# Two-layer cross attention on one core: the first layer's image-token softmax taken from the preparation into the attention's steps

## The reference

```
out_text = sdpa(q, k, v)                             # 1593 text tokens
out_ip   = sdpa(q, k_ip, v_ip, mask=mask_ip)         # 8 image tokens
out      = (out_text + out_ip) @ w_out + b_out + x   # the input of layer 2
```

## Time and profile before

| what | before |
|---|---|
| median of 3 runs | 1550.36 us (1549.09 to 1551.30) |
| the profiled execution's own time | 1552.15 us |
| its span in the profile | 1550.2 us |
| PE busy | 1456.7 us, 94% |
| DVE busy | 1119.9 us, 72% |
| ACT busy | 1060.8 us, 68% |
| POOL busy | 188.8 us, 12% |
| mean granted clock of PE, share of full | 0.969 |

### The profile page before, as it was taken

The page is one execution under the profiler, slowest core; times in us unless marked ns, Lnnn a source line. Parts: engine busy times, 40 slices in busy tenths (PEclk is TensorE's granted clock), DMA queues, the critical chain, the costliest instruction groups (busy, mean ns, idle before and its releaser), DMA issues. The chain is left out here.

```text
span 1550.2 us, 32737 instructions
## 1 busy us (share of the span) xinstructions
PE 1456.7 (94%) x12886; PEld 911.9 (59%) x12886; DVE 1119.9 (72%) x1572; ACT 1060.8 (68%) x1962; POOL 188.8 (12%) x363
## 2 busy tenths in 40 slices
PE   6797959999999999999999999999999999999995
PEld 4454513333333333477777777777777777777774
DVE  5777768887787877876767777777777777777625
ACT  2454538877877877767767777777777777777752
POOL 4653300000101101000010000000000000000000
PEclk9899959999999999899999999999999999999996
DMA  5266851221221212110011101100011001100000
GB/s 158 75 161 174 226 115 48 53 51 40 58 54 47 66 40 51 42 26 23 17 26 30 29 19 26 26 23 20 23 26 26 22 18 27 26 23 16 7 1 17
DMA packets 82902, 75.89 MB, mean 49 GB/s; under 512 B 28608, under 2 KB 70964, under 8 KB 82756
## 3 DMA queue, kind: packets, MB, share of 16 engines
q1 hardware_dynamic: 82756, 73.88, 18.3%
HBM read 47.73 MB, written 26.09 MB: 48 GB/s over the span
## 5 line engine op out<-in xcount | busy, mean ns | idle before, releaser
L1364 DVE TENSOR_TENSOR whole<-late,whole 128x1024 f16<-128x1024 f32 (+1 forms) x280 | 320.1, 1143 | 99.3 <-ACT whole L1223 96.2
L1349 DVE TENSOR_REDUCE mx<-ps_y 128x2 f32<-128x800 f32 (+2 forms) x227 | 223.9, 986 | 106.1 <-PE ps_y L1030 105.4
L1107 PE MATMUL ps_v<-eh,whole 128*128 128x269 f16 x1040 | 293.1, 282 | 0.0
L1107 PE MATMUL ps_n<-eh,whole 128*128 128x269 f16 x1040 | 291.6, 280 | 0.0
L1223 ACT CAST whole<-late 128x1024 f16<-128x1024 f32 (+1 forms) x280 | 275.6, 984 | 8.9
L1109 PE MATMUL ps_v<-el,whole 128*128 128x269 f16 x960 | 269.1, 280 | 0.0
L1110 PE MATMUL ps_v<-eh,whole 128*128 128x269 f16 x960 | 269.1, 280 | 0.0
L1110 PE MATMUL ps_n<-eh,whole 128*128 128x269 f16 x960 | 268.2, 279 | 0.0
L1109 PE MATMUL ps_n<-el,whole 128*128 128x269 f16 x960 | 268.1, 279 | 0.0
L1349 DVE TENSOR_REDUCE mx<-ps_x 128x2 f32<-128x800 f32 (+2 forms) x198 | 195.3, 987 | 82.0 <-PE ps_x L1030 81.1
L1349 DVE TENSOR_REDUCE mx<-ps_t 128x2 f32<-128x800 f32 (+2 forms) x215 | 211.4, 983 | 32.8 <-PE ps_t L1030 31.9
(11 more groups left out here) (433 smaller groups left out, 2072.9 us busy)
## 6 DMA issues: line engine op xcount, KB each, us to landing
e<-in_ctx SPq DMA_DIRECT2D x4, 1536.0 KB
kb<-k_parts SPq DMA_DIRECT2D x80, 74.9 KB
kb<-k_parts SPq DMA_DIRECT2D x80, 74.7 KB
k_parts<-kp SPq DMA_DIRECT2D x12, 400.0 KB
vb<-v_cols SPq DMA_DIRECT2D x40, 117.0 KB, 2.1
v_cols<-late SPq DMA_DIRECT2D x4, 1040.0 KB, 11.7
late<-v_cols SPq DMA_DIRECT2D x40, 104.0 KB, 2.0
qb<-q_parts SPq DMA_DIRECT2D x160, 25.0 KB
```

Source lines behind the costliest of these rows:

```text
L1107: pe.matmul(ps, hi, eh, start=(t == 0), stop=False)
L1349: nc.vector.tensor_reduce(mx[:, pair % 2, c, :], bank("max", pair, c)[:, :, 0:w], AX.X, ALU.max).then_inc(chunk_max, 1)
L1364: nc.vector.tensor_tensor(pl[s % 2][:, t0:t0 + w, :], ring[:, turn % EXPS, 0:w], ph[s % 2][:, t0:t0 + w, :], ALU.subtract).then_inc(low_do ...
```

## The change

`sc` of layer 0 leaves `queries` as before, but neither DVE nor ACT touches it in the preparation. In `attend` DVE makes one of the six operations at the end of each of steps 2, 3, 4, 6, 7 and 8, behind the reduce of p = 14 and ahead of the next step's p = 1; ACT makes the exponential at the end of step 5, behind the exponential of p = 12 and ahead of the copy in line 1256. An operation waits for the one before it by a semaphore; the reciprocal and the others keep their shapes. PE waits for the last of them ahead of stage `pT`. `mask` now lives as long as `sc`, and maximum and sum have small tiles of their own.

```diff
 STAGE0 = 1
+SOFTMAX_AT = (2, 3, 4, 6, 7, 8)
+EXP_SC_AT = 5
...
-                    if first:
-                        act.wait_ge(centred, 1)
-                        nc.scalar.activation(L["sc"][:], L["sc"][:], ACT.Exp).then_inc(exp_done, 1)
...
-                centre(nc.vector, link, L, 0, L["mask"], smax).then_inc(centred, 1)
...
-                    if first:
-                        dve.wait_ge(exp_done, 1)
-                        link(normalise(nc.vector, link, L, 0, None, ssum))
...
+        centring, exp_sc, norming = sem("centring"), sem("exp_sc"), sem("norming")
+        smax, ssum = sbuf("smax_0", [P, U * H], F32), sbuf("ssum_0", [P, U * H], F32)
+        sc0 = LS[0]["sc"][:].rearrange("p u (h n) -> p (u h) n", n=IP[0])
...
                     if name == "pT":
+                        pe.wait_ge(norming, 3)
...
+                    if s == EXP_SC_AT:
+                        act.wait_ge(centring, 3)
+                        nc.scalar.activation(LS[0]["sc"][:], LS[0]["sc"][:], ACT.Exp).then_inc(exp_sc, 1)
                     if stage_at(s):
...
+                def small_softmax(j):
+
+                    wide = [P, U * H, IP[0]]
+                    if j < 3:
+                        at_least(dve, centring, j)
+                    else:
+                        at_least(dve, norming, j - 3)
+                    if j == 0:
+                        for u in range(U):
+                            rows = LS[0]["sc"][:, u].rearrange("p (h n) -> p h n", n=IP[0])
+                            ins = nc.vector.tensor_tensor(rows, rows, LS[0]["mask"][:, u].to_broadcast([P, H, IP[0]]), ALU.add)
+                    elif j == 1:
+                        ins = nc.vector.tensor_reduce(smax[:], sc0, AX.X, ALU.max)
+                    elif j == 2:
+                        ins = nc.vector.tensor_tensor(sc0, sc0, smax[:].unsqueeze(2).to_broadcast(wide), ALU.subtract)
+                    elif j == 3:
+                        dve.wait_ge(exp_sc, 1)
+                        ins = nc.vector.tensor_reduce(ssum[:], sc0, AX.X, ALU.add)
+                    elif j == 4:
+                        ins = nc.vector.reciprocal(ssum[:], ssum[:])
+                    else:
+                        ins = nc.vector.tensor_tensor(sc0, sc0, ssum[:].unsqueeze(2).to_broadcast(wide), ALU.mult)
+                    ins.then_inc(centring if j < 3 else norming, 1)
...
                     low(s, NE - 1)
+                    if s in SOFTMAX_AT:
+                        small_softmax(SOFTMAX_AT.index(s))
                     if stage_at(s):
```

More of the change, by code:

```diff
@@ L122, in build @@
             ))
+        LS[0].update(mask=sbuf("mask", [P, U, 1, IP[0]], F32))
         LS[1].update(
@@ L131, in build @@
             L.update(parts=(sbuf("qp0", [P, 3, U * P], BF16, st), sbuf("qp1", [D - P, 3, U * P], BF16, st)),
-                     no_max=sbuf("no_max", [MROWS * H, U * P], BF16, st), mask=sbuf("mask", [P, U, 1, IP[0]], F32, st),
+                     no_max=sbuf("no_max", [MROWS * H, U * P], BF16, st),
                      vaug=vaug, vcut=vcut,
@@ L293, in prepare @@
         vh_done = sem("vh_done")
-        centred, exp_done, sm_step = sem("centred_0"), sem("exp_done_p"), sem("sm_step")
-        smax = K["res"][:, RR * KC:RR * KC + U * H]
-        ssum = K["n2"][:].rearrange("p g h -> p (g h)")[:, 0:U * H]
         eh_done, el_done = sem("eh_done"), sem("el_done")
@@ L1424, in centre @@
     sc = L["sc"]
[L1425 to L1431, removed]
+    link(vec.tensor_tensor(sc[:], sc[:], extra[:].rearrange("p u h n -> p u (h n)"), ALU.add))
     flat = sc[:].rearrange("p u (h n) -> p (u h) n", n=n)
```

## The result

The changed kernel takes **1554.29 us** (median of 10 runs, 1552.17 to 1558.50), the kernel before it 1550.34 in the same comparison (10 runs). The ratio is **1.0040**, with a 95% interval of 1.0028 to 1.0051: 4.3 to 7.9 us slower, 6.2 in the middle. The two medians lie 4.0 apart and the means of the two sets of ten 5.6; each set is spread over some 6 us, so the size is known no better than the interval says. The profiled execution took 1552.87 with a span of 1551.1.

The account below looks back on a forecast made before the run. The preparation was taken as a chain of waits, the attention as three engines passing work round three PSUM tiles. 6.36 + 0.7 - 2.5 = +4.6 us on the median 1550.36 gave 1555.0, range 1550.0 to 1558.8.

Parts of the forecast that it names:

- The two terms: Whole kernel: the preparation gets 2.5 us shorter, and the operations put into the attention add 7.06 us.
- The preparation: Batches 0 and 1: POOL's subtractions come earlier without DVE's softmax; gain 2.5 us, of which 1.6 from the front.
- Rival 2: Preparation: the softmax's two-input DVE operations hold POOL's first all-reduce, so up to 4.9 us comes back; 1552.6 us, chance 0.14.
- The attention: Steps 2 to 8: six DVE operations cost 6.36 us and ACT's exponential 0.7.
- the cover read from step 39: Attention, end of a step: slack before PE's score fill is late hides 0.37 us of each inserted DVE operation.
- ACT's exponential: Attention, end of step 5, ahead of ACT's copy: 1.18 us net, predicted cost 0.7, bounds 0 and 1.18.
- the two-step check in the prediction: Attention, plain step against step 39: reduce to score fill takes 2.55 us in both, so 0.36 inserted cost nothing.
- the granted clock: Attention steps with an operation: a fall below full clock would prove the forecast wrong; no size given.
- the bounds for the six operations: Attention: the six DVE operations cost between nothing (all covered by idle time) and 8.58 us (no cover).
- Rival 1: Attention: DVE's idle time, 1.5 us a step, covers the operations; 0 added, 2.5 gained, 1547.9 us, chance 0.13.

## Why the prediction was right

**The sign and the size.** It gave 4.6 us over the kernel before; measured are 6.2 (4.3 to 7.9). The 1555.0 lies 0.7 above the median of the changed kernel. The two terms that it had come to 6.7 - 2.6 = 4.1 by the runs, a little under that interval; the rest of the 6.2 fits a term that it left out (below).

**The preparation** (2.5 predicted, 2.6 measured with the softmax left out). The chain is the predicted one: the all-reduce stays behind POOL's configuration change (50.44, not 48), the second right behind it, the subtraction 1.8 earlier (1.6), ACT's first cast of batch 1 at 88.56 (89.5). Rival 2 is out with the first of these. The other profiles agree. From the first all-reduce to the first subtraction it is 9.56 to 9.95 in the three with the softmax in its old place and 7.66 to 8.02 in seven with it out; from that subtraction to batch 1's it is 39.18 to 40.00 and 38.46 to 39.01. That is 1.9 and 0.8 in the mean, where 1.6 and 0.9 were reckoned. The 6.1 by which the attention starts earlier in the two profiles is mostly the profiled execution of the kernel before. From DVE's first `eh` memset (38.58 there) to the attention's first `xT` memset (205.92) that execution took 167.3. The two profiles of the kernel with the operations made twice, which has the same preparation, took 163.2 and 163.5. Seven profiles with the softmax out of the preparation took 159.8 to 162.2, 161.3 in the mean: 2.1 less than these two. Most of the other 4.0 came in batches 2 and 3 of that one execution, where ACT's key casts wait for the landing of key DMAs.

**The attention** (7.06 predicted, 6.68 at full clock). The table has it term by term. The operations, each its duration less 0.08 and 0.37, came within 0.13 of every row at full clock, so the cover read from step 39 holds for whole operations. The one term off by more is ACT's exponential, 0.42 for 0.70. The prediction has the exponential behind the copy 0.89 late; it starts 2.32 after the last one of the step (274.86 to 277.18), in a plain step 1.66 (257.75 to 259.41), so it is 0.66 late. And PE's one wait of any size there isn't at that fill, but for the copy, at the product:

```profile
277.35 0.62 PE L1071 MATMUL ps_v<-whole,vb 128*9 128x256 f32 x8 [0.57 <-ACT acc L1245]
```

What the two-step check in the prediction could not see is that nothing is caught up later: only 0.14 comes back in the step behind the product.

**The term that was missing** is the granted clock. The sum took all steps at full clock. The text named a fall as something that would make it wrong, because no row had a stall of that length, but gave it no price; the bounds for the six operations ended at 8.58. It cost 1.3 to 2.7 in three of four profiles, 1.4 in the mean of the four; 4.1 and 1.4 make 5.5, within the interval. That the total came near without this term is in part luck: the spread of the runs is wider than the term, and an exponential 0.28 too dear made up for a little of it.

**Rival 1** failed for the place that the change chose, not in general. DVE's 1.5 us of idle time a step is real. In pieces put where it lies, the whole softmax cost nothing that shows (0.02 in steps 2 to 9).

## What to carry to other kernels

Where several engines pass tiles round a ring, an inserted operation cost its length less the waiting time at its own place, whatever the busy share of the engine said; read that place's gap from the timeline and cut the work to its size. What a step gives back is bounded by the next thing that isn't moved, here the time that another engine took from one kind of operation to the next, so look for the wait that will open there. Compare starts of stages over several profiles before a difference of two is taken for the change's: here 4 of 6 us were one execution's.

## What the runs showed of the hardware

- The granted clock fell to half after PE had waited 1.63 us in an otherwise busy stretch, in three of four profiles, and not in the fourth, after 1.62; once in twenty waits of 1.14 or 1.15; and after waits of 4.67 and of 3.85. In the kernels where PE never waited 0.9 us in steps 2 to 9 (softmax left out, behind the fold, in pieces) it stayed full. PE then worked at 1.2 GHz for about 3 to 8 us. What else decides it isn't shown.
- A two-input DVE operation of 1.49 us on SBUF held back a POOL subtraction that began under it by 1.2 us (2.15 to DVE's next block instead of 0.96); a one-input reduce of the same length, which also writes less, did not (1.05). The Trainium skill, SBUF — State Buffer, Who interferes with whom, says that a DVE instruction with two SBUF inputs contends with a GpSimd instruction that reads SBUF and that a tensor_reduce never does; these two rows agree.
- From the end of batch 0's all-reduce to POOL's next subtraction it was 6.86 to 7.30 us in all these profiles, and 5.2 to 5.6 ahead of the first all-reduce, with nothing shown that POOL waited for. With the softmax gone from DVE, these distances set when the subtractions of batches 0 and 1 came (ahead of batch 1's all-reduce it was 5.84 to 6.49 without a wait shown), and so only 1.9 and 0.8 came back of the 4.95 and 4.1 us taken from DVE. In batches 2 and 3 the all-reduce waited for DVE.
